# Reading w2 from its float32 source in every token group instead of from a bf16 copy, and a fourth pair of query/key chunks placed three steps earlier

## The reference

```python
x = x + attn(layernorm(x))        # 16 heads of 64, causal softmax
x = x + ffn(layernorm(x))

def attn(x):                       # W_qkv [16,1024,192], W_out [16,64,1024]
    q, k, v = split(einsum('bsd,ndh->bnsh', x, W_qkv), 3)
    p = softmax(q @ k.T / sqrt(64) + causal_mask)
    out = (p @ v).reshape(B, -1, S)
    return einsum('bds,nhd->bsd', out, W_out)

def ffn(x):                        # w1 [1024,4096], w2 [4096,1024], float32
    return relu(x @ w1 + b1) @ w2 + b2
```

## Time and profile before

| | us |
|---|---|
| median of 2 runs | 1326.66 (1321.72 and 1331.6) |
| the profiled execution | 1325.03 |
| its span on the slowest core, 4 | 1323.5 |
| outside the span | 1.5 |
| spans of the other cores | 1304.5 to 1322.4 |
| granted TensorE clock, cores | 0.868 to 0.885 |

### The profile page before, as it was taken

How to read it: one execution, slowest core, us unless ns; L and a number is a source line. 1 busy time by engine, 2 the same in 40 slices (tenths; PEclk the granted TensorE clock), 3 DMA queues, 4 the chain that set the end, 5 groups by cost and what they waited for, 6 DMA issues and landing times.

```text
span 1323.5 us, 12730 instructions; the slowest of 8 cores (1304.5 to 1323.5 us)
## 1 busy us (share of the span) xinstructions
PE 966.5 (73%) x4566; PEld 391.4 (30%) x4656; DVE 472.6 (36%) x638; ACT 411.4 (31%) x443; POOL 46.2 (3%) x59
## 2 busy tenths in 40 slices
PE   1279787685858585877755467874999689977997
PEld 0134322221312131322211223332444334433443
DVE  0542334626363645444443522301351134212401
ACT  0134086575747575666666100001000100010000
POOL 2100200000000000000000001010000000000000
PEclk9989899796969697988867788897999789988999
DMA  8910810010100002000200299998434553445433
GB/s 192 183 9 1 71 17 8 1 17 0 17 1 1 0 0 33 0 1 1 32 0 1 71 172 189 229 208 243 134 106 146 154 161 96 144 137 165 128 128 128
DMA packets 107005, 109.98 MB, mean 83 GB/s; under 512 B 40384, under 2 KB 81344, under 8 KB 106944
## 3 DMA queue, kind: packets, MB, share of 16 engines
q0 software_dynamic: 47232, 25.24, 16.1%
q1 hardware_dynamic: 26432, 50.36, 12.3%
q10 hardware_dynamic: 33280, 33.56, 8.0%
HBM read 109.20 MB, written 25.17 MB: 102 GB/s over the span
## 4 chain that ended last, share of the span: by engine, by line
PE 61%; DMA 17%; DVE 13%; issue 4%; ACT 3%; DVEq 2%; POOL 0%; ACTq 0%; POOLq 0%; SPq 0%
PE arena L721 15%; PE arena L790 13%; PE arena L522 10%; PE arena L379 9%; PE arena L467 5%; DMA w2stage<-w 5%; DVE tmp_sb L631 5%; PE arena L301 4%; DMA wstage<-w1b 3%; DVE oscr_sb L538 3%; DVE x_sb L642 3%; DMA wstage<-wqkv 2%; DMA wstage<-wout 2%; DMA wstage<-w 2%; PE arena L482 2%
## 5 line engine op out<-in xcount | busy, mean ns | idle before, releaser
L495 ACT ACTIVATE p_sb<-arena,cst_sb 128x1024 bf16<-128x1024 f32 (+1 forms) x320 | 290.9, 987 | 95.4 <-PE arena L467 58.9
L522 PE MATMUL arena<-p_sb,vaug_h 128*128 128x512 bf16 (+3 forms) x611 | 182.8, 380 | 151.1 <-DVE oscr_sb L538 95.1
L721 PE MATMUL arena<-lnf_sb,wstage 128*128 128x512 bf16 x1000 | 232.3, 393 | 70.4 <-DMA wstage<-w1b 47.4
L790 PE MATMUL arena<-w2stage,h_sb 128*128 128x512 bf16 x1004 | 224.7, 382 | 17.8 <-DMA w2stage<-w 12.7
L735 DVE TENSOR_SCALAR h_sb<-arena,b1c_sb 128x512 bf16<-128x512 f32 x128 | 96.1, 751 | 217.0 <-PE arena L721 217.0
L721 PEld LDWEIGHTS arena<-lnf_sb,wstage 128*128 128x128 bf16 x1024 | 102.6, 101 | 199.0 <-issue 87.4
L790 PEld LDWEIGHTS arena<-w2stage,h_sb 128*128 128x128 bf16 x1024 | 99.9, 98 | 142.6 <-issue 26.4
L379 PE MATMUL arena<-lnf_sb,wstage 128*128 128x512 bf16 x502 | 122.5, 397 | 7.9 <-DMA wstage<-wqkv 6.4
L467 PE MATMUL arena<-qpair,kpair 64*128 64x512 bf16 (+3 forms) x640 | 124.4, 385 | 4.8 <-DVE kpair L402 4.8
L522 PEld LDWEIGHTS arena<-p_sb,vaug_h 128*128 128x128 bf16 x640 | 42.7, 100 | 207.0 <-issue 205.6
L395 DVE CAST qpair<-arena 64x512 bf16<-64x512 f32 x64 | 43.7, 682 | 144.2 <-PE arena L379 143.4
(11 more groups left out here) (37 smaller groups left out, 394.3 us busy)
## 6 DMA issues: line engine op xcount, KB each, us to landing
w2stage<-w2b SPq DMA_DIRECT2D x48, 512.0 KB, 3.7
wstage<-w1b ACTq DMA_DIRECT2D x24, 1024.0 KB, 5.4
x_sb<-x SPq DMA_DIRECT2D x4, 2048.0 KB, 14.6
wstage<-w POOLq DMA_DIRECT2D x8, 1024.0 KB, 12.3
w1b<-wstage ACTq DMA_DIRECT2D x8, 1024.0 KB, 7.8
w2stage<-w POOLq DMA_DIRECT2D x16, 512.0 KB, 10.8
w2b<-w2stage SPq DMA_DIRECT2D x16, 512.0 KB, 9.0
y<-y_sb SPq DMA_DIRECT2D x16, 512.0 KB, 4.2
```

Source lines behind the costliest of these rows:

```text
L495: e.activation(AP(p_sb, (si_ % 3) * 1024, [[3 * 1024, 128], [512, 2], [1, w_]]), AP(arena, b_ + off_, [[AR, 128], [512, 2], [1, w_]]), AF. ...
L522: e.matmul(AP(arena, (4 + hx) * 512 + off_, [[AR, 128], [1, w_]]), vaug_h[:, hx, j_ * 128:(j_ + 1) * 128], AP(p_sb, (si_ % 3) * 1024 + hx ...
L721: (lambda s_, dc_, fb_, wp_: lambda e: e.matmul(bankap(fb_, TF), AP(wstage, s_ * 1024 + dc_ * 512 + wp_ * 128, [[8 * 1024, 128], [1, 128]] ...
L790: (lambda s_, ww_, c2_, dh_, t_: lambda e: e.matmul(bankap(t_, 512), h1_sb[:, ww_, 128 * c2_:128 * (c2_ + 1)], w2stage[:, s_, 512 * dh_:51 ...
```

## The change

The scratch tensor `w2b` is gone. POOL loads every w2 buffer from the float32 `w2` in all four groups, and waits only for the last matmul on that buffer. SP neither writes nor reads a copy, and keeps only the `y` stores. Apart from that, the fourth place of `ck_slots` moves from 35 to 32.

```diff
-    w2b_d = nc.dram_tensor("w2b", [W1N, D], BF16, kind="Internal")
...
-            ck_slots = {8, 17, 26, 35} if next_chunks else set()
+            ck_slots = {8, 17, 26, 32} if next_chunks else set()
...
-                    wfree = w2q_free[wq]
-                    wfree = wfree if isinstance(wfree, list) else [wfree]
-                    if g == 0:
-                        add("gpsimd",
...
-                            waits=wfree, inc=f"dv{wq}", amt=16)
-                        dwp = (f"dv{wq}", C[f"dv{wq}"])
-                        ds2 = add("sync",
-                                  (lambda sp_, ww_: lambda e: e.dma_start(
-                                      AP(w2b_d, ww_ * 128 * D,
-                                         [[D, 128], [128 * D, 2], [1, D]]),
-                                      AP(w2stage, sp_ * 1024,
-                                         [[8 * 1024, 128], [1024, 2],
-                                          [1, 1024]])))(sp2, ww),
-                                  waits=[dwp], inc=f"dt{wq}", amt=16)
-                        w2wb[wq] = (f"dt{wq}", ds2)
-                    else:
-                        add("sync",
-                            (lambda sp_, ww_: lambda e: e.dma_start(
-                                AP(w2stage, sp_ * 1024,
-                                   [[8 * 1024, 128], [1024, 2], [1, 1024]]),
-                                AP(w2b_d, ww_ * 128 * D,
-                                   [[D, 128], [128 * D, 2], [1, D]])))(
-                                sp2, ww),
-                            waits=wfree, inc=f"dk{wq}", amt=16)
-                        dwp = (f"dk{wq}", C[f"dk{wq}"])
+                    add("gpsimd",
+                        (lambda sp_, ww_: lambda e: e.dma_start(
+                            AP(w2stage, sp_ * 1024,
+                               [[8 * 1024, 128], [1024, 2], [1, 1024]]),
+                            AP(w2_d, ww_ * 128 * D,
+                               [[D, 128], [128 * D, 2], [1, D]])))(sp2, ww),
+                        waits=[w2q_free[wq]], inc=f"dv{wq}", amt=16)
+                    dwp = (f"dv{wq}", C[f"dv{wq}"])
...
                 if ww % 2 == 1:
-                    wq2 = (ww // 2) % 4
-                    w2q_free[wq2] = ([("mm", mm_t), w2wb[wq2]] if g == 0
-                                     else ("mm", mm_t))
+                    w2q_free[(ww // 2) % 4] = ("mm", mm_t)
```

More of the change, by code:

```diff
@@ L52, in build_program @@
         C[f"dh{_i}"] = 0
-    for _i in range(4):
-        C[f"dt{_i}"] = 0
-        C[f"dk{_i}"] = 0
     def vdrain():
@@ L666, in build_program @@
         w2q_free = [("mm", 0)] * 4
-        w2wb = [None] * 4
         out_bank_free = []
@@ L746, in build_program @@
                     sp2 = wq * 2
-                    wfree = w2q_free[wq]
-                    wfree = wfree if isinstance(wfree, list) else [wfree]
-                    if g == 0:
-                        add("gpsimd",
-                            (lambda sp_, ww_: lambda e: e.dma_start(
-                                AP(w2stage, sp_ * 1024,
-                                   [[8 * 1024, 128], [1024, 2], [1, 1024]]),
-                                AP(w2_d, ww_ * 128 * D,
-                                   [[D, 128], [128 * D, 2], [1, D]])))(
-                                sp2, ww),
-                            waits=wfree, inc=f"dv{wq}", amt=16)
-                        dwp = (f"dv{wq}", C[f"dv{wq}"])
-                        ds2 = add("sync",
-                                  (lambda sp_, ww_: lambda e: e.dma_start(
-                                      AP(w2b_d, ww_ * 128 * D,
-                                         [[D, 128], [128 * D, 2], [1, D]]),
-                                      AP(w2stage, sp_ * 1024,
-                                         [[8 * 1024, 128], [1024, 2],
-                                          [1, 1024]])))(sp2, ww),
-                                  waits=[dwp], inc=f"dt{wq}", amt=16)
-                        w2wb[wq] = (f"dt{wq}", ds2)
-                    else:
-                        add("sync",
-                            (lambda sp_, ww_: lambda e: e.dma_start(
-                                AP(w2stage, sp_ * 1024,
-                                   [[8 * 1024, 128], [1024, 2], [1, 1024]]),
-                                AP(w2b_d, ww_ * 128 * D,
-                                   [[D, 128], [128 * D, 2], [1, D]])))(
-                                sp2, ww),
-                            waits=wfree, inc=f"dk{wq}", amt=16)
-                        dwp = (f"dk{wq}", C[f"dk{wq}"])
+                    add("gpsimd",
[6 more added lines that the diff above has]
+                    dwp = (f"dv{wq}", C[f"dv{wq}"])
                 s, dww = sp2 + (ww % 2), dwp
@@ L851, in build_program @@
                                  ("dsb0", C["dsb0"]), ("dsb1", C["dsb1"])] +
-                          [(f"dt{i}", C[f"dt{i}"]) for i in range(4)] +
-                          [(f"dk{i}", C[f"dk{i}"]) for i in range(4)] +
                           [(f"dy{i}", C[f"dy{i}"]) for i in range(4)] +
```

## The result

| | before | after |
|---|---|---|
| median | 1324.33 us (10 runs) | 1312.34 us (11 runs) |
| ratio of the changed kernel to before | | 0.9891, 95% interval 0.9856 to 0.9925 |
| the profiled execution, span | 1325.03, 1323.5 | 1311.43, 1309.9 |
| spans of the cores | 1304.5 to 1323.5 | 1285.8 to 1309.9 |

What follows compares the result with a forecast made beforehand. Transfers were taken to bound FFN2 of group 0 and the start of groups 1 to 3, TensorE FFN2 of groups 1 to 3. -14 + 4.5 - 7.5 + 0 = -17.0 us from 1325.0 gave 1308 us, range 1286 to 1332.

Steps and rivals of the forecast that it cites:

- the gap: Bias row to next FFN1: first w1b quad waits less beside leftover float32 loads than four bf16 ones; -7.5 us over three.
- the chunks: Attention: moving the fourth pair three steps earlier moves ACT's idle hole without closing it; 0 us, bounds -3.5 and +3.5.
- FFN2 of group 0: Removing 16 copy writes and the wait for them makes TensorE the bound; -14 us, bounds -16.8 and -1.9.
- FFN2 of groups 1 to 3: Float32 loads at 3.7 us a buffer land slightly late, 1.5 us per group; +4.5 us, bounds 0 and +44.7.
- The 2 us given back for lateness: FFN2 of group 0: some 2 us of lateness over the formula's 0.6, for loads and w1b writes still under way.
- three signs of being wrong: FFN2 of group 1 over 60 us; quad wait under 9 or over 16 us; pass changed by over half a microsecond.
- Rival 1: Loads keep up in every group's FFN2 and quads come quickly at the boundaries; -40, 1285 us, chance 0.22.
- rivals 2 and 3: Second: group 0 gain kept, rest cancels, 1320 us, chance 0.17. Third: device memory gives out in FFN2, 1371 us, 0.09.
- Rival 4: Attention: DVE casts fall clear of the epilogue, saving half a microsecond a pass; 1305 us, chance within the forecast's 0.52.

Runs made afterwards that it cites:

- the quads behind FFN1: Changed kernel with fourth chunk place back at 35, plus next group's first two w1b quads issued behind FFN1; 0.9598 of the kernel before, median 1279.16 us.
- chunks alone: The kernel before with only the fourth pair of chunks moved from 35 to 32; 1.0084 of the kernel before.
- no copy: Group 0 as in the changed kernel, no w2 copy written; groups 1 to 3 load bf16 through SP from w1b (wrong weights); 0.9872 of the kernel before.
- the w2 part alone: The changed kernel with the fourth pair of chunks back at place 35; 0.9833 of the kernel before.
- three buffers: Changed kernel with fourth chunk place back at 35 and three w2 buffers in rotation instead of four; 0.9858 of the kernel before.
- the w2 loads held back: Changed kernel, fourth chunk place at 35, first four w2 loads of groups 1 to 3 waiting for FFN1's second quad; 0.9945 of the kernel before.

## Why the prediction was right, and which steps weren't

The total came out within 3 us, and that is in part luck. Two terms came out 3 and 4.5 us better than forecast, and the gap and the chunks 3 and at least 8 us worse. The chunks are the step that was wrong; the others are sizes.

| term | forecast | measured, and by what |
|---|---|---|
| FFN2 of group 0 | -14 | -17: all cores at 55.4, mean before 72.3 |
| FFN2 of groups 1 to 3 | +4.5 | 0: the profile after |
| gap before FFN1, three times | -7.5 | -4 to -5: means of the cores, 20.3 before, 18.7 after |
| chunks | 0 | +8 to +12: three pairs of kernels |
| sum | -17 | -14 by the ratio; the terms give -14 to -9 |

**FFN2 of group 0.** Right in mechanism: the DMA engines bounded it, the write of the copy was 23.4 us of them, and without it TensorE bounds. The copy written but unread leaves it at 73.3 us, no copy with bf16 loads brings 55.4. The 2 us given back for lateness were not needed.

**FFN2 of groups 1 to 3.** The pace was right, 3.51 us a buffer against 3.55 worked out from the earlier trace rows. The time to landing was mis-sized: 8.3 us was the minimum of group 0, where the loads ran beside writes; without them the median is 6.5. A shortest value out of a crowded stage is no lower bound for an empty one. The term was 1.5 us too high in each group. The figure of the Trainium skill (HBM Reference, Specifications), from which a buffer would be read in an estimated 2.9 us, is not reached: 3.51 us of engine time are 299 GB/s of reading. Its conclusion, that nothing is late, held.

**The gap.** What was to lie beside the quads does: on core 0 one float32 load was under way when the first quad was issued, and the quad took 11.8 us where 12.4 was forecast. Those w2 loads cost 5 us, and the `y` stores, for which the prediction had no price, as much (18.9 us to 14.1). But the difference that was to come from replacing bf16 loads by the rest of float32 ones isn't there: 18.7 us with either once no copy is written. The smaller mean gap was forecast for a reason that the runs don't support, from one core whose gap was among the longest.

**The chunks.** The failed step is "The hole moves and isn't closed ... 0 us, bounds -3.5 and +3.5". The arithmetic of ACT and PE holds: a short pass takes 71.5 us with 32 as with 35. It left out TensorE's clock, and put the step at nothing by that arithmetic alone; the runs showed +8 to +12 us. With the chunks at 32, 39 passes of 168 are long; with 35, in nine kernels, 6 of 504, each the second pass of its core, none after. The clock that the text called full speed in FFN2 was never looked at in attention, though the page has a row for it over the whole span.

Of the three signs of being wrong that the prediction named, one came true: passes that change by over half a microsecond. Rival 1 described the transfers rightly in FFN2 and wrongly at the gap; rivals 2 and 3, the slow paces, are out for these kernels. Rival 4 had the wrong sign.

## What to carry to other kernels

Before keeping a bf16 copy in device memory, price its write in the stage that makes it, not only the reads it saves: here it cost 17 us where the engines were full, and the reads that it halved cost nothing in FFN2 in either form. A transfer that is moved off one wait falls on the next unless the stage it goes to has both engine time and slack, so look for a stage that computes for long on weights already there, as with the quads behind FFN1 (31 us). And an edit that leaves every busy time alone can still cost 10 us by the clock: compare the length of repeated passes over all cores, not their mean.

## What the runs showed of the hardware

**The clock holds a rhythm.** With the chunks at 32 most long passes come in rows of two or four, and the work in them is the same. In the short passes of core 4 above the clock is at 1.00 from 20 us after the start to the end, through waits of PE of 1.5, 1.3 and 1.6 us; in the long ones of core 6, with waits of 1.5, 1.3 and 1.1 us at these places, it falls behind the first, for 3.4 us, and behind the second, for 6.8. A fall doesn't always cost: many short passes, as one of 71.6 us on core 3 from 510.1 us on, have the clock at 0.50 once more, from 47.7 to 51.1 us after their start:

```profile
557.80:561.20 3.40, 3.06 (x8) 0.48 (x8) 0.93 (x3) 3.09 (x3) 0.00 (x0) 0.51 0.00 0
```

What decides whether a wait brings the clock down isn't settled; that the share of long passes goes from 1% to 23% with the place of 16 matmuls is.

**The neighbouring core.** In the kernels with bf16 loads the gap goes with how far apart cores 4 and 5, or 0 and 1, reach it. In the profile before, cores 4 and 5 pass the bias row 3.8 us apart:

```profile
901.08 1.90 PE L806 MATMUL arena<-b2r_sb,ones_sb 1*128 1x512 bf16 x8
...
924.20 6.00 PE L721 MATMUL arena<-lnf_sb,wstage 128*128 128x512 bf16 x21 [16.20 <-DMA wstage<-w1b]
```

this is core 5, with 23.1 us, and core 4 has 23.1 too (904.90 to 927.96, above). The other pairs that near, 3.8 to 5.8 us, are the two further boundaries of these cores and the first of cores 0 and 1, with 21.6 to 23.1 us. At distances of 11 us or more, in 18 pairs of before, chunks alone and no copy, it is 18.0 to 19.7 us but for one of 20.5. So the 23 us on the slowest core, from which the prediction started, were probably in part its neighbour's, and the gap of a single profile is no price. No run changes the distance alone, and the near cases are four boundaries of one execution, so this is argued and not shown. The Trainium skill (HBM Reference, Specifications) says that two cores share one memory's bandwidth; the trace fits this for these neighbours, by 4 us a gap. With float32 loads distances of 4 to 7 us showed 17.7 to 20.3 us in the changed kernel and the w2 part alone, no more than far ones there (16.7 to 20.7 from 8 us on), and up to 21.2 with three buffers.

**A clock of 0.81 under full load.** In the profile with the w2 loads held back, cores 6 and 7 ran FFN2 of group 0 in 67.3 us with no wait in it, the other six in 55.4. Core 6:

```profile
848.00:858.00 10.00, 10.00 (x39) 4.13 (x38) 0.00 (x0) 0.00 (x0) 1.66 (x3) 0.81 0.78 124
```

PE is busy throughout, at 0.81 in place of 1.00. This is a third level, seen in this profile alone, on these two cores in FFN1 and FFN2 of group 0; it is left out of the account above.
